# Sinks' product stacked in 48 rows, and the farthest key block turned together with the own block

## The reference, cut to what matters

```python
WINDOW = 512
SINK = 4
causal = j <= i
band = j >= i - (WINDOW - 1)
mask = causal & band
mask = mask | (j < SINK)
...
att = jnp.einsum('bkgqd,bkjd->bkgqj', q, k) * scale
att = jnp.where(mask[None, None, None, :, :], att, -jnp.inf)
att = jax.nn.softmax(att, axis=-1)
y = jnp.einsum('bkgqj,bkjd->bkgqd', att, v)
```

## Time and profile before

| | |
|---|---|
| Median of 3 runs | 2277.97 us (2277.34 to 2278.72) |
| Profiled execution | 2280.01 us |
| Its span, from first to last instruction | 2278.1 us |
| TensorE busy | 2201.2 us (97%) |
| VectorE busy | 1465.0 us (64%) |
| ScalarE busy | 862.7 us (38%) |
| GpSimd busy | 148.3 us (7%) |
| Mean share of the transfer engines on the main queue | 46.2% |

### The profile page before, as it was taken

The page is one execution under the profiler, slowest core; times in us unless marked ns, Lnnn a source line. Parts: engine busy times, 40 slices in busy tenths (PEclk is TensorE's granted clock), DMA queues, the critical chain, the costliest instruction groups (busy, mean ns, idle before and its releaser), DMA issues. The chain is left out here.

```text
span 2278.1 us, 36251 instructions
## 1 busy us (share of the span) xinstructions
PE 2201.2 (97%) x13769; PEld 1629.9 (72%) x13769; DVE 1465.0 (64%) x3071; ACT 862.7 (38%) x1837; POOL 148.3 (7%) x337
## 2 busy tenths in 40 slices
PE   7999999999999999999999999988999999999998
PEld 6766666767666677666676766656888888888886
DVE  6465666555667756566665556575666766667667
ACT  2254554434555435455443545463111111111111
POOL 2000001000001000000100000000010000100100
PEclk9999999999999999999999999999999999999999
DMA  6486459533546734445863354555233243342431
GB/s 250 154 265 200 129 188 285 171 114 112 165 153 219 251 122 144 143 134 177 278 199 110 116 199 147 210 172 192 99 141 132 107 147 103 136 141 98 147 122 63
DMA packets 173358, 366.55 MB, mean 161 GB/s; under 512 B 12424, under 2 KB 110856, under 8 KB 158880
## 3 DMA queue, kind: packets, MB, share of 16 engines
q1 hardware_dynamic: 168240, 348.30, 46.2%
q0 software_dynamic: 4544, 14.75, 1.9%
q10 hardware_dynamic: 432, 1.57, 0.2%
HBM read 284.79 MB, written 79.72 MB: 160 GB/s over the span
## 5 line engine op out<-in xcount | busy, mean ns | idle before, releaser
L766 ACT ACTIVATE pt<-t_ps 128x512 f32<-128x512 f32 x480 | 266.0, 596 | 515.6 <-PE t_ps L1047 514.0
L980 PE MATMUL j_ps<-x_hi,w 128*128 128x512 f32 x1232 | 414.3, 405 | 0.0
L775 ACT ACTIVATE probs<-probs,neg_max 128x660 f32<-128x660 f32 (+5 forms) x512 | 357.5, 703 | 45.0 <-DVE neg_max L1294 44.9
L1294 DVE CUSTOM_DVE_ANT_0 probs<-s_ps,mask 128x660 f32<-128x660 f32 (+5 forms) x512 | 322.4, 667 | 74.1 <-PE s_ps L1015 69.7
L1683 PE MATMUL out_ps<-wo,w 128*128 128x512 f32 x1536 | 355.1, 390 | 4.0 <-DVE w L1740 4.0
L1683 PEld LDWEIGHTS out_ps<-wo,w 128*128 128x128 f32 x1536 | 289.4, 188 | 64.7 <-issue 4.4
L1047 PE MATMUL t_ps<-ident,probs 128*128 128x128 f32 x1920 | 269.5, 279 | 25.4 <-DVE x_lo L1282 12.5
L1683 PE MATMUL gate_ps<-x_hi,w 128*128 128x512 f32 x1024 | 281.5, 391 | 4.8 <-PEq L442 4.8
L980 PEld LDWEIGHTS j_ps<-x_hi,w 128*128 128x128 f32 x1232 | 232.0, 190 | 53.6 <-issue 6.9
L1047 PEld LDWEIGHTS t_ps<-ident,probs 128*128 128x128 f32 x1920 | 208.3, 141 | 76.6 <-issue 47.7
L1015 PE MATMUL s_ps<-k_hi,q 64*128 64x330 f32 (+5 forms) x1664 | 247.2, 333 | 8.8 <-DVE q L1266 5.7
(11 more groups left out here) (178 smaller groups left out, 2190.5 us busy)
## 6 DMA issues: line engine op xcount, KB each, us to landing
fw<-in_L_ffn_d_w_dram SPq DMA_DIRECT2D x128, 1024.0 KB, 5.3
w<-WT SPq DMA_DIRECT2D x36, 1024.0 KB, 5.2
w<-XS SPq DMA_DIRECT2D x64, 512.0 KB, 6.4
XS<-x_hi SPq DMA_DIRECT2D x32, 512.0 KB, 7.1
XS<-x_lo SPq DMA_DIRECT2D x32, 512.0 KB, 8.1
Y<-y SPq DMA_DIRECT2D x256, 64.0 KB, 2.3
b_x<-in_L_attn_x_dram SPq DMA_DIRECT2D x32, 512.0 KB, 4.2
b_y<-Y SPq DMA_DIRECT2D x32, 512.0 KB, 6.5
```

The source lines that it names most:

```text
L766: act.activation(pt[:, m % PT_SLOTS, :, :], bank[:, :].rearrange("p (h q) -> p h q", q=P), ACT.Copy).then_inc(pt_ready, 1)
L775: act.activation(probs[:, slot, 0:width], probs[:, slot, 0:width], ACT.Exp, bias=neg_max[:, slot:slot + 1], scale=-1.0, accum_out=row_sum[ ...
L980: last = pe.matmul(bank_of((kind, b, n)), w[:, slot, wp * C + c * P:wp * C + c * P + P], xs[:, c, bass.ts(ch, BANK)], start=i == 0, stop=i ...
L1294: dve.tensor_tensor_reduce(out=probs[:, slot, 0:width].rearrange("p (a n) -> p a n", a=parts), in0=s_ps[head % 2][:, :].rearrange("p (a n) ...
```

## The change

1. Units with qb of 5, 6 and 7 turn one block fewer. The farthest block and the own block have complementary triangles, so VectorE adds them into the own block's place (`merge`, four additions of 128x128), divides 528 columns in place of 660, TensorE turns four blocks, and GpSimd splits the turned block into the two again (`split_merged`, two selects over 128x512 in `pt`). `values` takes the blocks in the order 1, 2, 3, 0, 4, and waits for the split before 0.
2. The sinks' probabilities are packed as high, low and high part (48 columns), turned into 48 rows, and multiplied with the sinks' values as high, high and low part, in one product of the fast format with 128 output rows for both halves. `pt_sink` and `sink_cols` are single now. The sinks' values are loaded by 12 transfers in place of 4 and split by ScalarE and VectorE once a batch in step 4.
3. At the start `own_head` (three instructions of GpSimd) becomes `own_pair` (one reduction of VectorE), and the bias rows of the feed-forward part are one copy in place of four.

The diff, cut to its core:

```diff
+def is_merged(qb):
+    return qb > WB
+def taken_of(qb):
+    return blocks_of(qb) - is_merged(qb)
 def turns_of(qb):
-    return blocks_of(qb) + has_sink(qb)
+    return taken_of(qb) + has_sink(qb)
...
-        SINKS = GROUP * SINK
+        SINKS = 3 * GROUP * SINK
...
-                    for head in range(GROUP):
-                        pool.dma_start(v_sink[SINK * head:SINK * head + SINK, :, :].rearrange("p (m g) d -> p m g d", g=2),
-                                       v_parts(b, 0)[0:SINK]).then_inc(v_sink_ready, 16)
+                        pool.wait_ge(v_sink_ready, b)
+                    for part in range(3):
+                        for head in range(GROUP):
+                            row, half = 64 + GROUP * SINK * part + SINK * head, head % 2
+                            pool.dma_start(v_raw[row:row + SINK, :, HS * half:HS * half + HS],
+                                           v_parts(b, 0)[0:SINK, :, half, :]).then_inc(v_sink_loaded, 16)
+
+                def split_merged(u):
+
+                    own = pt[:, (blocks_before(u) + WB) % PT_SLOTS, :, :]
+                    both = pt[:, blocks_before(u) % PT_SLOTS, :, :]
+                    pool.wait_ge(pt_ready, taken_before(u) + 1)
+                    pool.wait_ge(pv_done, u)
+                    pool.affine_select(out=own, in_=both, compare_op=ALU.is_ge, fill=0.0, base=0,
+                                       pattern=[[0, GROUP], [1, P]], channel_multiplier=-1).then_inc(pt_split, 1)
+                    pool.wait_ge(pt_split, 2 * packed_before(u) + 1)
+                    pool.affine_select(out=both, in_=both, compare_op=ALU.is_ge, fill=0.0, base=-1,
+                                       pattern=[[0, GROUP], [-1, P]], channel_multiplier=1).then_inc(pt_split, 1)
 
                 def pack_sinks(u):
                     slots = slice(GROUP * (u % 2), GROUP * (u % 2) + GROUP)
                     pool.wait_ge(normed, GROUP * u + GROUP)
-                    if u >= 2:
-                        pool.wait_ge(turned, turns_before(u - 1))
-                    pool.tensor_copy(sink_cols[u % 2][:, :, :], probs[:, slots, WIDE:WIDE + SINK]
-                                     ).then_inc(sinks_packed, 1)
+                    pool.wait_ge(turned, turns_before(u))
+                    raw = probs[:, slots, WIDE:WIDE + SINK]
+                    pool.tensor_copy(sink_cols[:, 0:3:2, :, :], raw.unsqueeze(1).to_broadcast([P, 2, GROUP, SINK])
+                                     ).then_inc(sinks_high, 1)
+                    pool.wait_ge(sinks_high, packed_before(u) + 1)
+                    pool.tensor_tensor(sink_cols[:, 1, :, :], raw, sink_cols[:, 0, :, :].bitcast(F32), ALU.subtract
+                                       ).then_inc(sinks_packed, 1)
...
+                        if (b or s) and is_merged((s - 1) % TB):
+                            split_merged(UNITS * b + s - 1)
                         if s == 2:
                             v_sinks(b)
...
+                    if s == WB:
+                        act.wait_ge(v_sink_loaded, 16 * 3 * GROUP * (b + 1))
+                        act.activation(v_sink[sink_rows, :, :], v_raw[sink_rows, :, :], ACT.Copy).then_inc(v_sink_high, 1)
...
+                    block = WB if is_merged(qb) and i == 0 else i
                     for head in range(GROUP):
                         last = pe.transpose(t_ps[(turns_before(u) + i) % 2][:, bass.ts(head, P)],
-                                            probs[:, GROUP * (u % 2) + head, PADDED * i:PADDED * i + P], ident[:, :])
+                                            probs[:, GROUP * (u % 2) + head, PADDED * block:PADDED * block + P], ident[:, :])
...
-                    for i in range(turns_of(qb)):
-                        wait_taken(u, i)
+                    order = (1, 2, 3, 0, 4) if is_merged(qb) else range(n)
+                    for i in order:
+                        if is_merged(qb) and i in (0, WB):
+                            pe.wait_ge(pt_split, 2 * packed_before(u) + 2)
+                        else:
+                            wait_taken(u, i)
...
+                    if has_sink(qb):
+                        wait_taken(u, taken_of(qb))
+                        last = pe.matmul(o_ps[:, 0:2 * P], v_sink[sink_rows, m, :],
+                                         pt_sink[sink_rows, :, :].rearrange("p a q -> p (a q)"), start=False, stop=True)
                     last.then_inc(pv_done, 1)
...
+                def merge(b, s, head):
+
+                    slot = GROUP * (UNITS * b + s) % (2 * GROUP) + head
+                    own = probs[:, slot, WB * PADDED:WB * PADDED + P]
+                    dve.tensor_tensor(own, own, probs[:, slot, 0:P], ALU.add).then_inc(merged, 1)
...
-                    width = width_of(qb)
                     slot = GROUP * (u % 2) + head
+                    part = slice(PADDED if is_merged(qb) else 0, width_of(qb))
...
+                def divide_pair(b, s, pair):
+                    invert(b, s, pair)
+                    for head in range(2 * pair, 2 * pair + 2):
+                        if is_merged(unit_of(s)[1]):
+                            merge(b, s, head)
+                    for head in range(2 * pair, 2 * pair + 2):
+                        divide(b, s, head)
...
                 def take_sinks(u):
 
-                    n = turns_before(u) + blocks_of(u % TB)
+                    n = turns_before(u) + taken_of(u % TB)
+                    dve.wait_ge(turned, n + 1)
+                    dve.wait_ge(pv_done, u)
...
-                    invert(b, s, 0)
-                    divide(b, s, 0)
-                    divide(b, s, 1)
+                    divide_pair(b, s, 0)
                     take_place(1)
                     if u and has_sink((u - 1) % TB):
                         take_sinks(u - 1)
-                    invert(b, s, 1)
-                    divide(b, s, 2)
-                    divide(b, s, 3)
+                    divide_pair(b, s, 1)
...
+                    if s == WB:
+                        dve.wait_ge(v_sink_high, b + 1)
+                        dve.tensor_tensor(v_sink[low_rows, :, :], v_raw[low_rows, :, :],
+                                          v_sink[low_rows, :, :].bitcast(F32), ALU.subtract).then_inc(v_sink_ready, 1)
```

More of the change, by code:

```diff
@@ L133, in turns_before, with taken_before @@
     return (KV * b + s // TB) * whole + sum(turns_of(qb) for qb in range(s % TB))
+def taken_before(u):
+    b, s = divmod(u, UNITS)
+    whole = sum(taken_of(qb) for qb in range(TB))
+    return (KV * b + s // TB) * whole + sum(taken_of(qb) for qb in range(s % TB))
 def blocks_before(u):
@@ L211, in attend @@
         bias_rows = small_rows[64:64 + B, 0:C]
-        pt_sink = [small_rows[96:96 + SINKS, BANK * n:BANK * n + BANK].rearrange("p (h q) -> p h q", h=GROUP)
-                   for n in range(2)]
-        v_sink = small_rows[96:96 + SINKS, C:C + KV * HS].rearrange("p (g d) -> p g d", d=HS)
-        own_head = sb("own_head", [SINKS, GROUP])
-        sink_cols = [sb(f"sink_cols{n}", [P, GROUP, SINK]) for n in range(2)]
+        sink_rows = slice(64, 64 + SINKS)
+        low_rows = slice(96, 96 + GROUP * SINK)
+        v_raw = small_rows[:, C:C + 2 * P].rearrange("p (m n) -> p m n", m=2)
+        v_sink = sb("v_sink", [P, 2, P], F32R)
+        pt_sink = sb("pt_sink", [P, 2, P], F32R)
+        own_pair = sb("own_pair", [SINKS, 2])
+        sink_cols = sb("sink_cols", [P, 3, GROUP, SINK], F32R)
         affine = sb("affine", [P, 4, KB])
-        d1_bias_rows = sb("d1_bias_rows", [P, HB, B])
+        d1_bias = sb("d1_bias", [P, HB])
         h_pre = sb("h_pre", [P, HB, B])
@@ L842, in _ @@
                         step(b, s)
-                for i in range(WB + 1):
+                for i in range(taken_of(TB - 1)):
                     take_turned(UNITS * B - 1, i)
@@ L1073, in values @@
                     if s == WB + 1:
-                        pe.wait_ge(v_sink_ready, 16 * GROUP * (b + 1))
-                    for i in range(turns_of(qb)):
-                        wait_taken(u, i)
-                        for half in range(2):
-                            if i < n:
-                                lhs = v[:, m * (1 + b % 2), qb - n + 1 + i, half, :]
-                                rhs = pt[:, (blocks_before(u) + i) % PT_SLOTS, :, :]
-                            else:
-                                lhs, rhs = v_sink[:, 2 * m + half, :], pt_sink[u % 2]
-                            last = pe.matmul(o_ps[HS * half:HS * half + HS, 0:2 * P], lhs, rhs[:, half::2, :],
-                                             start=i == 0, stop=i == turns_of(qb) - 1)
+                        pe.wait_ge(v_sink_ready, b + 1)
+                    order = (1, 2, 3, 0, 4) if is_merged(qb) else range(n)
[4 more added lines that the diff above has]
+                            wait_taken(u, i)
+                        for half in range(2):
+                            last = pe.matmul(o_ps[HS * half:HS * half + HS, 0:2 * P],
```

(13 more changed lines are left out.)

48 lines of the change are left out of this document (23 added, 25 removed).

## The result

The changed kernel takes 2239.17 us (median of 5 runs, 2235.07 to 2244.84) where the kernel before takes 2277.97 (5 runs, 2276.72 to 2278.72): ratio 0.9839, 95% interval 0.9818 to 0.9860. That is 38.8 us less, where 31 were forecast. Two more comparisons of the same pair gave ratios of 0.9841 (0.9819 to 0.9862) and 0.9830 (0.9805 to 0.9854).

A forecast was written before the change was run, and what follows sets the result against it. TensorE's queue in the attention stage was taken to bound most steps. Savings of 42.0 us, less 6.1 and 3.0 in tight units and 2 for contention, gave 31: from 2277.97 to 2247 us, range 2236 to 2262.

The forecast's parts named there:

- What bounds the kernel: Attention stage: TensorE's own queue sets the pace in most steps, VectorE's chain of mask, exponential, division in a few.
- the ones named: Units 22 and 23 of each batch and 29, 30, 31 of the last: 11 tight units, losing 6.1 and 3.0 us.
- The turn and the product: TensorE, each of 48 units with sinks: four turnings fewer and a cheaper sinks' product save 0.875 us, 42.0 in all.
- the lower bound: Sinks' product on TensorE: a change of shape after it cuts its saving from 0.45 to 0.31 us, total 35.3.
- VectorE's chain, +0.35 a unit: VectorE, units with sinks: added sums, less shorter divisions and sinks' copy, plus a 0.05 wait, lengthen the chain 0.35 us.
- Contention of GpSimd, 2 us, 0 to 10: GpSimd's selects and VectorE hold each other up in SBUF, costing 2 us in all, bounds 0 to 10.
- rival 2: Selects block VectorE's sums and divisions, each chain grows 0.62 to 1.24 us: 2261, to 2270 us; chance 0.16.
- The reason I gave for a small term: Early in a step VectorE mostly reads PSUM, so GpSimd's selects should meet little; 2 us taken.
- The split is hidden: GpSimd's pair of selects, 1.3 to 2.4 us with waits, fits in 7.7 us of room before block 0 in unit 22.
- Rival 3: TensorE waits for the split amid its values if a select takes over 3.8 us; 2297 us at 5 each; chance 0.03.
- Rival 1: Cover holds everywhere, as ScalarE's missing copy lets VectorE start earlier in tight steps: all 42.0 us gained, 2236; chance 0.1.
- Rival 4: Waits on the sinks' single buffers hold the queue and give the gain back: 2270 to 2282 us; chance 0.07.

## Why the prediction was right, and where it was off

- **What bounds the kernel**: right. Steps with room gave all that TensorE lost; the steps without are the ones named.
- **The turn and the product** (0.425 + 0.45 per unit): right, though the one change of shape that a run isolates costs 0.20 and not 0.135. Alone they give 0.45 and 0.46, together 0.91, 1.2 us more than forecast over 37 units. The second change of shape, the lower bound, doesn't come; the run with 128 rows shows it.
- **VectorE's chain, +0.35 a unit**: this term was mis-sized; it measured 0.00. I charged each pair of sums at 0.42 us and saw no cover; the handover from the reciprocal to the first division covered 0.15 of each. Against the full 0.875, steps 22 and 23 lost 0.46 and 0.90 us instead of 0.82 and 1.22: 3 x 0.69 = 2 us better than the forecast. In the last batch the tight units lost 2 us, not 3.
- **Contention of GpSimd, 2 us, 0 to 10**: 0. The mechanism of rival 2 exists, but a meeting costs at most 0.45 us and not 0.62, and the selects never meet a sum or division in this order of work. The reason I gave for a small term was the right one.
- **The split is hidden**: right. The 7.7 us from its start to the fourth block were 7.2 in unit 22, where 5.8 are left behind its end; elsewhere 4.2 to 14.3 are left, and 1.5 in the last unit. Rival 3's mechanism is real, as the run with fourteen selects shows; with a split of 10.3 us the cost was 142 us.
- **Rival 1** (all 42 us, 2236) is nearer in the total, but its mechanism isn't there: steps 22 and 23 of the first three batches gained 0.42 and nothing, not 0.875 each. What brought the time down to 2239 is in the terms above.
- **Rival 4**: no single-buffer wait gave the gain back. The wait for the sinks' copy grew from 2.5 to 4.6 us; in units 22 and 23 of the first three batches VectorE's later divisions end last anyway.

Of the 7.8 us by which the forecast fell short, the steps account for 1.2 + 2.1 + 1 + 2 = 6.3.

## What to carry to other kernels

An instruction that doesn't need the result before it can run in the handover to the one that does; cost it by what it adds to the chain between two starts, not by its own length. Before you give work to GpSimd, see what VectorE does in that stretch: here selects cost nothing beside readers of PSUM, and up to 0.45 us for each sum or division from SBUF to SBUF that they met. When a chain is made shorter by moving a piece of it forward, ask of that piece in each step whether its own input is there yet; one step in which it isn't can cost the gain of the others.

## What the runs showed that I had not expected

The granted clock falls for a few microseconds at a time, and each such stretch in a step costs about 1.5 us (step 1 of a batch takes 6.77 us without and 8.28 or 8.29 with one, in the traces of the changed kernel). It is no property of the kernel alone. Two traces of the same changed kernel, in step 1 of the second batch (columns as in the earlier trace rows, the clock third from the right). First the last trace taken, whose turning of unit 1 starts at 476.20:

```profile
466.00:470.00 4.00, 4.00 (x40) 3.04 (x34) 1.14 (x5) 1.40 (x5) 1.69 (x3) 1.00 0.09 19
470.00:474.00 4.00, 4.00 (x17) 3.24 (x18) 3.33 (x17) 1.28 (x6) 4.00 (x8) 0.57 0.11 20
```

and the first one, where it starts at 479.50:

```profile
474.00:478.00 4.00, 4.00 (x28) 3.31 (x27) 2.67 (x15) 1.71 (x8) 4.00 (x8) 1.00 0.18 37
```

A mean of 0.57 over four microseconds is most of them at the lower level, 1.2 of 2.4 GHz, and TensorE had been busy without a gap in the four before. Between the first and the last turning, three traces of the changed kernel have three, one and seven of these stretches; they come at the same places of the program, in steps 1, 24 and 28, and not each time. The one in step 24 comes right behind two waits of 0.76 and 0.73 us, for the sinks' copy and the divisions of unit 23, which stand close together only since the change; it fell there once in three batches of the first trace, never in the second, three times in the third. What decides it is open. Single runs of the changed kernel therefore spread over 11 us (2233.86 to 2244.84), which is more than most of the effects measured here; the distances between turnings in two traces agree within 0.1 us outside of these stretches, except in steps 11 and 30 of the last batch (0.5 each), and the small effects here are read from them.
